# A depthwise convolution on four engines: a third ScalarE tap that goes into PSUM under TensorE's two, and sums of h taken where it is written

## What is computed

```python
x = x + dilation(group_norm(x))                      # 11 x 11 morphological dilation
x = x + L1_conv(group_norm(x), ...)                  # what the change is in
```

```python
out = jnp.einsum('oi,bihw->bohw', proj_w[:, :, 0, 0], x) + proj_b[None, :, None, None]
h = jax.lax.conv_general_dilated(out, dw_w, window_strides=(1, 1), padding=((1, 1), (1, 1)),
                                 feature_group_count=C, ...)      # 3 x 3 depthwise
h = h + dw_b[None, :, None, None]
mean = h.mean(axis=(0, 2, 3))
var = h.var(axis=(0, 2, 3))
h = (h - mean) * rsqrt(var + BN_EPS) * bn_g + bn_b ; h = gelu(h)
# then offsets from h by a 1 x 1 convolution and tanh, and a bilinear resampling of x
```

## Time and profile before

| | us |
|---|---|
| runs before (three) | 11152.15, 11159.74, 11159.03 |
| median | 11159.03 |
| the profiled execution, its own time | 11149.29 |
| its span in the trace | 11147.4 |
| first projection of the convolution, start | 9220.8 |
| first VectorE step of the convolution's first window | 9231.9 |
| first VectorE step of the second window, of the last one | 9259.5, 10099.2 |
| end of the last step on h, end of the last sum | 10125.8, 10138.2 |

### The profile page before, as it was taken

One profiled execution on the slowest core, in us unless ns is written; L12 is line 12 of the kernel. 1 busy time (PEld: TensorE's weight loads), 2 busy tenths in 40 slices (PEclk: granted clock), 3 DMA queues, 4 the chain that ended last, 5 costly groups with the idle time before them and its releaser, 6 DMA issues. The chain is left out here.

```text
span 11147.4 us, 74869 instructions
## 1 busy us (share of the span) xinstructions
PE 8347.9 (75%) x16532; PEld 3201.8 (29%) x16532; DVE 10631.9 (95%) x5882; ACT 9898.5 (89%) x7193; POOL 9104.7 (82%) x2891
## 2 busy tenths in 40 slices
PE   1777777777777777777777777777777777886665
PEld 0222222222222222222222222222222223332222
DVE  8999999999999999999999999999999998998999
ACT  2999999999999999999999999999999987776666
POOL 2888888888888888888888888888888885666777
PEclk9999999999999999999999999999999998998888
DMA  7666666666666666666666666666666663444555
GB/s 286 128 128 129 129 129 129 129 128 128 128 128 128 129 125 126 128 128 128 125 129 127 129 125 128 127 128 126 129 128 128 126 120 157 159 160 168 212 213 213
DMA packets 386979, 1573.30 MB, mean 141 GB/s; under 512 B 20944, under 2 KB 127568, under 8 KB 324432
## 3 DMA queue, kind: packets, MB, share of 16 engines
q0 software_dynamic: 218256, 901.04, 44.9%
q1 hardware_dynamic: 168256, 667.25, 16.0%
HBM read 465.90 MB, written 201.33 MB: 60 GB/s over the span
## 5 line engine op out<-in xcount | busy, mean ns | idle before, releaser
L446 POOL TENSOR_TENSOR m_pool<-r_pool,u 128x2048 f32<-128x2048 f32 x1536 | 6777.4, 4539 | 919.6 <-ACT r_pool L540 860.6
L495 PE MATMUL chain<-dx,mats 128*128 128x512 f32 x6144 | 3111.2, 649 | 952.9 <-ACT chain L558 951.9
L643 DVE SCALAR_TENSOR_TENSOR acc_a<-m_pool,kt,acc_a 128x2048 f32<-128x2048 f32 x1472 | 3465.7, 2354 | 60.2 <-POOL m_pool L446 17.7
L495 PE MATMUL chain<-dx,neg_ident 128*128 128x512 f32 x4608 | 2417.7, 672 | 851.0 <-ACT chain L558 850.6
L643 DVE SCALAR_TENSOR_TENSOR acc_a<-u,kt,acc_a 128x2048 f32<-128x2048 f32 x960 | 2261.2, 2355 | 31.9
L540 ACT ACTIVATE r_pool<-dx,gap_l 128x2048 f32<-128x2048 f32 x1024 | 2051.6, 2004 | 75.4 <-POOL m_pool L446 36.2
L495 PEld LDWEIGHTS chain<-dx,mats 128*128 128x128 f32 x6144 | 1167.2, 201 | 2896.7 <-ACT chain L558 1747.4
L643 DVE SCALAR_TENSOR_TENSOR acc_a<-t,kt,acc_a 128x2048 f32<-128x2048 f32 x768 | 1808.2, 2354 | 22.8
L558 ACT ACTIVATE chain<-chain,gap_r 128x1024 f32<-128x1024 f32 x1536 | 1631.0, 1089 | 110.6 <-PE chain L495 110.2
L495 PE MATMUL chain<-u,mats 128*128 128x512 f32 x3072 | 1457.9, 606 | 216.9 <-ACT chain L558 216.9
L495 PEld LDWEIGHTS chain<-dx,neg_ident 128*128 128x128 f32 x4608 | 919.5, 211 | 2348.8 <-ACT chain L558 1458.5
(11 more groups left out here) (144 smaller groups left out, 6976.5 us busy)
## 6 DMA issues: line engine op xcount, KB each, us to landing
t<-u POOLq DMA_DIRECT2D x768, 1059.0 KB, 8.7
u<-x_dram SPq DMA_DIRECT2D x28, 3328.0 KB, 27.5
xw<-x_scratch SPq DMA_DIRECT2D x64, 1152.0 KB, 6.9
hw<-h_scratch SPq DMA_DIRECT2D x66, 1024.0 KB, 8.9
x<-xc POOLq DMA_DIRECT2D x65, 1024.0 KB, 8.8
xt<-x_dram SPq DMA_DIRECT2D x32, 2048.0 KB, 14.4
xc<-x_dram SPq DMA_DIRECT2D x64, 1024.0 KB, 4.7
x_scratch<-x SPq DMA_DIRECT2D x64, 1024.0 KB, 9.8
```

The source lines that it names most:

```text
L446: nc.gpsimd.tensor_tensor(m_pool[j % MP][:], r_pool[j % RP][:], u[s][:, k * CR + di:k * CR + di + CR, base:base + W], ALU.add).then_inc(m_ ...
L495: added = nc.tensor.matmul(chain[h][:, r:r + 2, :], weight, src[:, top:top + 2, dj:dj + W], start=False, stop=True, skip_group_check=True)
L643: nc.vector.scalar_tensor_tensor(out=acc_a[:], in0=src, scalar=k_base, in1=acc_a[:], op0=ALU.subtract, op1=ALU.max).then_inc(a_done, 1)
```

## The change

In the convolution ScalarE takes three taps in place of two, and VectorE four in place of five. The third ScalarE tap (tap 8) is written straight into hp as a *seed*, before TensorE's two taps of the same part, which are added on top (`start=False`). So the order in a part is now ScalarE's seed, TensorE's taps, VectorE's chain. For the matmuls to add to what ScalarE wrote, TensorE writes both hp buffers once at the start (four matmuls, `hp_open`).

The sum of h is no longer a pass of its own. VectorE's last step and ScalarE's four tap operations each write the sum of what they produce (`accum_out`), into `part_sums` and `tap_sums`. The squares remain passes of ScalarE over h, now one for each part of four rows (1024 elements, `square`). At the head of `resample` two sums become three and two additions come in. The clearing of h[1] at the start goes.

ScalarE's order in a window is written anew (`begin`, `rest`): it fetches ahead into the next window. The cut diff, with "..." for what is left out:

```diff
-TAPS_PE, TAPS_ACT = 2, 2
+TAPS_PE, TAPS_ACT = 2, 3
...
+                for s in range(2):
+                    for r in range(0, QR, 2):
+                        opened = nc.tensor.matmul(hp[s][:, r:r + 2, :], ident,
+                                                  mats[:].rearrange("p (a b) n -> p a (b n)", a=2),
+                                                  start=True, stop=True, skip_group_check=True)
+                opened.then_inc(hp_open, 1)
...
                 def taps(n, s, q):
-                    pe.wait_ge(evacuated, n * NPROJ + (NPROJ + q + 3))
-
-                    pe.wait_ge(h_chain, n * DVE_STEPS + (DVE_STEPS + 1 + (q - 1) * CHAIN))
+
+                    pe.wait_ge(hp_seeded, n * PARTS + (q + 1))
...
-                                                    start=(t == 0), stop=(t == TAPS_PE - 1))
+                                                    start=False, stop=True, skip_group_check=True)
...
-                def sum_before(n, s, which):
-
-
-                    act.wait_ge(pool_adds, n * ADDS + 2 * ADDS)
-                    act.wait_ge(h_summed, n * 2 + (1 + which))
-                    passed(act, act_turns)
-                    nc.scalar.activation(waste[:], h[1 - s][:], (ACT.Identity, ACT.Square)[which],
-                                         bias=h_shift[:, 0:1],
-                                         accum_out=h_sums[:, which, bass.ds(n, 1)]).then_inc(h_summed, 1)
...
+                def seed(n, s, q):
+
+                    act.wait_ge(evacuated, n * NPROJ + (NPROJ + q + 3))
+
+                    act.wait_ge(h_chain, n * DVE_STEPS + (DVE_STEPS + 1 + (q - 1) * CHAIN))
+                    ty, tx = divmod(8, 3)
+                    nc.scalar.activation(hp[q % 2][:], o[s][:, q * QR + ty:(q + 1) * QR + ty, tx:tx + W], ACT.Identity,
+                                         bias=zero[:, 0:1], scale=par[:, COL_DW + 8:COL_DW + 9]).then_inc(hp_seeded, 1)
...
+                                         bias=zero[:, 0:1], scale=par[:, COL_DW + t:COL_DW + t + 1],
+                                         accum_out=tap_sums[:, 2 * half + which, bass.ds(n, 1)]).then_inc(act_taps, 1)
+
+                def square(n, s, q):
+
+                    act.wait_ge(pool_adds, n * ADDS + (2 * ADDS + 2 + 2 * (q // (PARTS // HALVES))))
+                    act.wait_ge(h_squared, n * PARTS + (PARTS + q + 1))
+                    passed(act, act_turns)
+                    nc.scalar.activation(waste[:], h[s][:, q * QR:(q + 1) * QR, :], ACT.Square,
+                                         bias=h_shift[:, 0:1],
+                                         accum_out=h_squares[:, q, bass.ds(n, 1)]).then_inc(h_squared, 1)
+
+                def begin(n, s):
+                    for e in range(3):
+                        evacuate(n, s, e)
+
+                def rest(n, s, squares, ahead):
+
+                    seed(n, s, 1)
+                    evacuate(n, s, 4)
+                    tap(n, s, 0, 0)
+                    if squares:
+                        square(n - 1, 1 - s, 0)
+                    seed(n, s, 2)
+                    evacuate(n, s, 5)
+                    tap(n, s, 0, 1)
+                    if squares:
+                        square(n - 1, 1 - s, 1)
+                    seed(n, s, 3)
+                    if ahead:
+                        begin(n + 1, 1 - s)
+                    tap(n, s, 1, 0)
+                    if ahead:
+                        seed(n + 1, 1 - s, 0)
+                        evacuate(n + 1, 1 - s, 3)
+                    tap(n, s, 1, 1)
+                    if squares:
+                        square(n - 1, 1 - s, 2)
+                        square(n - 1, 1 - s, 3)
...
-                nc.vector.memset(h[1][:], 0.0)
...
+                                    in1=hp[q % 2][:], op0=ALU.mult, op1=ALU.add,
+                                    accum_out=part_sums[:, q, bass.ds(n, 1)] if step_no == CHAIN - 1 else None) \
+                                    .then_inc(h_chain, 1)
```

More of the change, by code:

```diff
@@ L870, in tap @@
                                          o[s][:, lo + ty:lo + ty + HALF_ROWS, tx:tx + W], ACT.Identity,
-                                         bias=zero[:, 0:1],
-                                         scale=par[:, COL_DW + t:COL_DW + t + 1]).then_inc(act_taps, 1)
-                with nc.Fori(0, NWIN // 2, engines=ACT_ONLY) as i:
-                    for s in range(2):
-                        n = i * 2 + s
-                        act.wait_ge(h_chain, n * DVE_STEPS + 1)
-                        act.wait_ge(act_taps, n * (2 * HALVES) + 1)
-                        for e in range(4):
-                            evacuate(n, s, e)
-                        tap(n, s, 0, 0)
-                        evacuate(n, s, 4)
-                        tap(n, s, 0, 1)
-                        evacuate(n, s, 5)
-                        sum_before(n, s, 0)
-                        tap(n, s, 1, 0)
-                        tap(n, s, 1, 1)
-                        sum_before(n, s, 1)
@@ L894, in _ @@
+                begin(0, 0)
+                seed(0, 0, 0)
+                evacuate(0, 0, 3)
+                rest(0, 0, False, True)
+                with nc.Fori(0, NWIN // 2 - 1, engines=ACT_ONLY) as i:
+                    for s in range(2):
+                        rest(i * 2 + (s + 1), 1 - s, True, True)
+                rest(NWIN - 1, 1, True, False)
+                for q in range(PARTS):
+                    square(NWIN - 1, 1, q)
             @block.gpsimd
@@ L1202, in _ @@
                 link(nc.vector.memset(tab[:], 1.0))
-                for t in range(2):
-                    link(nc.vector.tensor_reduce(mv[:, t:t + 1], h_sums[:, t, 1:], mybir.AxisListType.X, ALU.add))
-                nc.vector.tensor_scalar(mv[:], mv[:], 1.0 / (GROUPS * H * W), None, ALU.mult) \
-                    .then_inc(moments_ready, 1)
+                for t, sums in enumerate((part_sums, h_squares)):
+                    link(nc.vector.tensor_reduce(mv[:, t:t + 1], sums[:].rearrange("p q n -> p (q n)"),
+                                                 mybir.AxisListType.X, ALU.add))
+                link(nc.vector.tensor_reduce(cm[:, 0:1], tap_sums[:].rearrange("p q n -> p (q n)"),
+                                             mybir.AxisListType.X, ALU.add))
+                link(nc.vector.tensor_tensor(mv[:, 0:1], mv[:, 0:1], cm[:, 0:1], ALU.add))
+                link(nc.vector.tensor_scalar(mv[:], mv[:], 1.0 / (GROUPS * H * W), None, ALU.mult))
+                nc.vector.tensor_tensor(mv[:, 0:1], mv[:, 0:1], h_shift[:], ALU.add).then_inc(moments_ready, 1)
                 dve.wait_ge(means_ready, 1)
```

36 lines of the change are left out of this document (22 added, 14 removed).

## The result

The changed kernel takes **11213.59 us** (median of 5 runs, 11209.59 to 11215.05) against 11159.03 us: a ratio of 1.005, with a 95% interval of 1.0036 to 1.0065. It is slower by 54.6 us; the prediction was 11205, with a range of 11166 to 11265.

The account below looks back on a forecast made before the run. VectorE was taken to bound the convolution before; afterwards ScalarE's order, with a round trip through TensorE, gives 29.6 us a window against 27.99: +48 us over 30 windows, -2 at the ends, so 11205 us, range 11166 to 11265.

Follow-up runs that it names:

- both orders: Changed kernel with ScalarE's and TensorE's orders both rewritten so no ScalarE operation stands right behind what it waits for, same work: 10992.0 us, ratio 0.985 to the kernel before.
- the plain order with the third tap: Changed kernel without ScalarE's fetching ahead for the next window, its order in a window as in the kernel before: 11149.1 us (one run).
- the opening at the start of the stage: Changed kernel with both orders rewritten, plus TensorE's four opening matmuls moved from behind the tables to the stage's start: 10987.9 us, ratio 0.9849 to the kernel before.

## What to carry to other kernels

Before an engine is relieved, walk once round the window along every other engine in its own order, and ask at each operation whether what it waits for stands behind something of its own in another queue; a round trip costs the whole way there and back, however idle the engines are on average. A wait that was harmless while another engine was the bound becomes the bound when that engine is relieved, so a rebalancing and a new order belong together: here the same instructions took 11214 us in one order and 10992 in another. And ask what is late next at the ends of a stage too.

## What the runs showed of the hardware that was not expected

- A VectorE multiply-and-add of 1024 float32 elements that also writes its sum costs no time behind the operation (the 0.24 us in front of it stay unexplained): the read is an instruction of 0.08 us, and the next operation starts 1.20 us after the step's start, as without it. On ScalarE the read is 0.19 us long, and the next operation starts 0.09 to 0.10 us later than without it.
- TensorE's clock stayed up through short waits and often fell behind longer ones. In the eleven traces here, 529 groups of eight taps stand behind 1.0 to 1.96 us of idle time, and none was slow (3.70 us each at most). Of the 189 groups behind 2.78 to 3.05 us, 127 were slow (over 5 us), in the kernel before all 32, in the changed one 20 of 31. With the long waits gone the granted clock was 1.00 over 600 us of the stage, with both orders and in the plain order with the third tap as well, where TensorE is busy for only 483.58 us of it; it was 0.93 in the kernel before and 0.95 in the changed one.
- Matmuls run well before they are needed do not leave the clock up: after the opening at the start of the stage and a wait of 7.8 us with three small groups of matmuls between, the first projections took 8.69 us instead of 5.75, with the granted clock at 0.50 up to 9230.0 and 0.82 from there to 9234.6.
